# Projecting two chunks of batch 0's keys and values ahead of LayerNorm and the query projection

## The reference

```
x   (8, 64, 512)      ctx (8, 1601, 384)
xn  = layernorm(x)
q   = (xn @ Wq + bq), k = (ctx @ Wk + bk), v = (ctx @ Wv + bv)     # 16 heads of 32
x   = x + softmax(q k^T / sqrt(32)) v @ Wo + bo
x   = x + experts(layernorm(x))                                     # top 2 of 8, hidden 2048
```

## Time and profile before

| | us |
|---|---|
| median of three runs | 1233.47 |
| lowest and highest | 1231.24 and 1234.61 |
| the profiled execution | 1227.9 |
| its span in the trace | 1226.1 |
| PE busy | 1143.8 (93%) |
| DVE busy | 958.2 (78%) |
| ACT busy | 704.6 (57%) |
| POOL busy | 428.0 (35%) |

### The profile page before, as it was taken

How to read it: one execution, slowest core, us unless ns; L and a number is a source line. 1 busy time by engine, 2 the same in 40 slices (tenths; PEclk the granted TensorE clock), 3 DMA queues, 4 the chain that set the end, 5 groups by cost and what they waited for, 6 DMA issues and landing times.

```text
span 1226.1 us, 23151 instructions
## 1 busy us (share of the span) xinstructions
PE 1143.8 (93%) x7488; PEld 1054.2 (86%) x7489; DVE 958.2 (78%) x2082; ACT 704.6 (57%) x1418; POOL 428.0 (35%) x378
## 2 busy tenths in 40 slices
PE   4899999999999999999999998757889999889998
PEld 4799999999999999999999997635668898668897
DVE  6578888888888888888888888865876756876655
ACT  3456656656656656656656656443575565665654
POOL 5454754754654654654664640010000000000000
PEclk9899999999999999999999999966899999989999
DMA  5322122122122122122122103113755634655633
GB/s 181 101 63 62 40 70 61 38 70 61 38 70 61 38 70 61 38 70 61 39 69 61 58 23 118 50 52 105 244 189 184 206 109 164 221 191 193 201 117 103
DMA packets 74304, 121.15 MB, mean 99 GB/s; under 512 B 10776, under 2 KB 35480, under 8 KB 74272
## 3 DMA queue, kind: packets, MB, share of 16 engines
q1 hardware_dynamic: 74272, 120.73, 30.6%
HBM read 118.62 MB, written 2.10 MB: 98 GB/s over the span
## 4 chain that ended last, share of the span: by engine, by line
PE 79%; DVE 9%; ACT 5%; DMA 3%; issue 3%; DVEq 0%; SPq 0%; ACTq 0%
PE ps L401 18%; PE ps L403 17%; PE ps L402 17%; PE ps L1285 7%; PE ps L1337 7%; PE ps L1321 4%; PE ps L1322 3%; DMA w_raw<-in_w_dram 2%; PE ps L1386 2%; DVE w_lo L1027 2%; DVE mx L955 1%; DVE k_mix L877 1%; PE ps L1429 1%; DVE w_lo L1019 1%; PE ps L1430 1%
## 5 line engine op out<-in xcount | busy, mean ns | idle before, releaser
L545 POOL TENSOR_TENSOR ctx_hi<-ctx_raw,no_query 128x1152 fp32r<-128x1152 f32 x64 | 142.8, 2231 | 290.2 <-PE ps L403 281.2
L877 DVE SCALAR_TENSOR_TENSOR k_mix<-ps,bk_sb,k_mix 64x384 fp32r<-64x384 f32 (+1 forms) x256 | 162.3, 634 | 82.1 <-ACT k_mix L644 77.8
L684 ACT ACTIVATE probs<-ps,negmax 128x1152 f32<-128x1152 f32 x64 | 78.3, 1223 | 201.1 <-DVE negmax L958 201.1
L401 PE MATMUL ps<-wv_hi,ctx_hi 128*128 128x256 f32 (+1 forms) x624 | 181.8, 291 | 6.7 <-DVE k_mix L877 6.5
L549 POOL TENSOR_TENSOR ctx_lo<-ctx_raw,ctx_hi 128x1152 fp32r<-128x1152 f32 x64 | 179.7, 2808 | 5.0
L403 PE MATMUL ps<-wv_hi,ctx_lo 128*128 128x256 f32 (+1 forms) x624 | 175.7, 282 | 0.0
L402 PE MATMUL ps<-wv_lo,ctx_hi 128*128 128x256 f32 (+1 forms) x624 | 174.9, 280 | 0.0
L644 ACT ACTIVATE k_mix<-ps,bk_sb 64x384 fp32r<-64x384 f32 (+1 forms) x256 | 150.8, 589 | 24.0 <-PE ps L403 19.4
L969 DVE TENSOR_TENSOR pt_mix<-ps,pt_mix 128x384 fp32r<-128x384 f32 (+1 forms) x256 | 142.2, 580 | 1.4 <-ACT pt_mix L695 1.4
L401 PE MATMUL ps<-ctx_hi,wk_hi 128*128 128x384 f32 (+1 forms) x384 | 133.2, 347 | 0.0
L403 PE MATMUL ps<-ctx_hi,wk_lo 128*128 128x384 f32 (+1 forms) x384 | 132.3, 345 | 0.0
(11 more groups left out here) (219 smaller groups left out, 2668.5 us busy)
## 6 DMA issues: line engine op xcount, KB each, us to landing
w_raw<-in_w_dram SPq DMA_DIRECT2D x68, 1024.0 KB, 5.3
ctx_raw<-in_ctx_t_dram SPq DMA_DIRECT2D x48, 576.0 KB, 3.8
ctx_raw<-in_ctx_t_dram SPq DMA_DIRECT2D x16, 673.5 KB, 4.1
q_both<-q_scratch SPq DMA_DIRECT2D x14, 128.0 KB, 3.1
x<-in_x_dram SPq DMA_DIRECT2D x1, 1024.0 KB, 5.4
wq_raw<-in_wq_dram SPq DMA_DIRECT2D x1, 1024.0 KB, 7.7
q_scratch<-q_out SPq DMA_DIRECT2D x1, 1024.0 KB, 5.4
wo_raw<-in_wo_dram SPq DMA_DIRECT2D x1, 1024.0 KB, 5.4
```

Of the source, the lines that this page charges most:

```text
L401: pe.matmul(acc_ap, a_hi, b_hi, start=start, stop=False)
L545: nc.gpsimd.tensor_tensor(ctx_hi[slot][:, :, 0:n], ctx_raw[slot][:, :, 0:n], no_query[:].rearrange("p (o i) -> p o i", o=1).broadcast_to([ ...
L877: last = nc.vector.scalar_tensor_tensor(out=k_mix[other, 2 * a + i, cols], in0=ps[rows, bank, 0:m], scalar=bk_sb[rows, a:a + 1], in1=k_mix ...
```

## The change

Chunks 0 and 1 of batch 0 are projected first, and LayerNorm and q come after them; chunks 2 and 3 follow q as before. In detail:

- SP issues the biases, Wk, ctx chunk 0, Wv, ctx chunk 1, and then x and Wq. The second loads of chunks 0 and 1 are issued ahead of the store of q.
- ACT copies Wk, chunk 0, Wv and chunk 1 high (the chunks were POOL's), then takes the high parts of chunk 0's units, then Wq, unit 0 of chunk 1, the square root and the table of Exp, the other units of chunk 1, the turned blocks, and chunks 2 and 3, with `qbd_hi` after chunk 2.
- DVE makes Wk low, chunk 0 low, Wv low, then mixes LayerNorm's pieces between the low parts of the ten units; the turned blocks and q follow. `qbd_lo` comes after chunk 2.
- POOL makes chunk 1 low and Wq low (which was DVE's), then chunks 2 and 3.
- PE runs jobs 0 and 1, turns x, makes q, runs jobs 2 and 3. q goes to banks 5, 6, 4 and 7 (`q_bank`).
- The buffers of the start have other places, so that Wq, x and their parts lie where the first units don't write.

```
--- before
+++ after
         first, used[0] = ExitStack(), 0
+        wkv_raw = place("wkv_raw", [P, 2, KC, D], F32, first)
+        pad_to(4 * TILE0[2] * 2 * D, "first_pad0", first)
+        x0 = place("x0", [P, TT, D], F32, first)
+        xn0 = place("xn0", [P, TT, D], F32, first)
         wq_raw = place("wq_raw", [P, KD, D], F32, first)
+        pad_to(4 * (2 * KT * D + STEPS // 2 * NKE), "first_pad1", first)
...
+        def q_bank(m):
+            return (PROJ_BANK + 1, PROJ_BANK + 2, PROJ_BANK, PV_BANK)[m]
...
 # SP
+            sp.dma_start(bk_sb[:], bk_t).then_inc(bias_loaded, 16)
+            sp.dma_start(bq_sb[:], bq_t).then_inc(bias_loaded, 16)
+            sp.dma_start(bv_sb[:], bv_t).then_inc(bias_loaded, 16)
+            sp.dma_start(wkv_raw[:, 0], wk.rearrange("(k p) n -> p k n", p=P)).then_inc(wkv_loaded[0], 16)
+            load_ctx(0, 0, 0)
+            sp.dma_start(wkv_raw[:, 1], wv.rearrange("(k p) n -> p k n", p=P)).then_inc(wkv_loaded[1], 16)
+            load_ctx(0, 1, 1)
             sp.dma_start(x0[:], x_rows).then_inc(x_loaded, 16)
             sp.dma_start(wq_raw[:], wq.rearrange("(k p) n -> p k n", p=P)).then_inc(wq_loaded, 16)
...
 # POOL
             make_norm_tables()
-            for m in range(CHUNKS):
-                split_ctx(m + 1, m, 16 * (m // 2 + 1), UNIT0[m - 1] if m >= 2 else None)
+            pool.wait_ge(ctx_high, 2)
+            pool.wait_ge(ctx_split, 1)
+            nc.gpsimd.tensor_tensor(ctx_lo[1][:, :, 0:KEYS[1]], ctx_raw[1][:, :, 0:KEYS[1]],
+                                    ctx_hi[1][:, :, 0:KEYS[1]].bitcast(F32), ALU.subtract).then_inc(ctx_split, 1)
+            pool.wait_ge(wq_high, 1)
+            nc.gpsimd.tensor_tensor(wq_lo[:], wq_raw[:], wq_hi[:].bitcast(F32), ALU.subtract).then_inc(wq_split, 1)
+            for m in range(2, CHUNKS):
+                split_ctx(m + 1, m, 16 * (m // 2 + 1), UNIT0[m - 1])
...
 # ACT
+            split_first(wkv_raw[:, 0], wk_hi[:], wkv_loaded[0]).then_inc(wkv_high, 1)
+            split_first(ctx_raw[0][:, :, 0:KEYS[0]], ctx_hi[0][:, :, 0:KEYS[0]], ctx_loaded[0]).then_inc(ctx_high, 1)
+            split_first(wkv_raw[:, 1], wv_hi[:], wkv_loaded[1]).then_inc(wkv_high, 1)
+            split_first(ctx_raw[1][:, :, 0:KEYS[1]], ctx_hi[1][:, :, 0:KEYS[1]], ctx_loaded[1]).then_inc(ctx_high, 1)
...
             act.wait_ge(bias_loaded, 48)
-            for c in range(CHUNKS):
+            job_high(None, 0, range(UNITS[0]))
+            split_first(wq_raw[:], wq_hi[:], wq_loaded).then_inc(wq_high, 1)
+            job_high(None, 1, range(KEY_UNITS[0] + 1))
+            act.wait_ge(var_ready, 1)
+            nc.scalar.activation(sd[:], ve[:], ACT.Sqrt).then_inc(sd_ready, 1)
+            warm(ACT.Exp, 1)
+            job_high(None, 1, range(KEY_UNITS[0] + 1, UNITS[1]))
+            for k in range(KD):
+                act.wait_ge(xt_ready, k + 1)
+                nc.scalar.copy(xt0_hi[:, k, :], ps[:, k, :]).then_inc(xt_high, 1)
+            for c in range(2, CHUNKS):
                 job_high(None, c, range(UNITS[c]))
-                if c == 0:
+                if c == 2:
...
 # DVE
+            job_low(None, 0, KEY_UNITS)
+            dve.wait_ge(x_loaded, 16)
+            for t in range(TT):
+                last = nc.vector.bn_stats(stat[:, t, :], x0[:, t, :])
+            step(last)
+            job_low(None, 0, range(len(KEY_UNITS), UNITS[0]))
+            variance()
+            job_low(None, 1, KEY_UNITS[:1])
+            inverse_deviation(1)
+            job_low(None, 1, KEY_UNITS[1:])
+            normal_rows(x0, xn0)
+            job_low(None, 1, range(len(KEY_UNITS), UNITS[1]))
...
 # PE
+            for c in range(2):
+                for k in range(UNITS[c]):
+                    pe.wait_ge(wkv_split, 1 if k in KEY_UNITS else 2)
+                    run_job(None, c, [k])
+            turn(xn0, 0, TT)
+            pe.wait_ge(wq_split, 1)
+            pe.wait_ge(xt_split, KD)
+            pe.wait_ge(proj_split, UNIT0[2])
+            for m in range(KD):
...
+                    last = three_pass(pe, ps[:, q_bank(m), :], ...)
+                last.then_inc(q_ready, 1)
             pe.wait_ge(q_done, KD - 1)
-            for c in range(CHUNKS):
+            for c in range(2, CHUNKS):
                 run_job(None, c, range(UNITS[c]))
```

More of the change, by code:

```diff
@@ L435, in _ @@
                 load_ctx(0, m, m % 2)
+            for c in range(2):
+                sp.wait_ge(ctx_split, CHUNKS - 1 + c)
+                load_ctx(0, c, c % 2)
             sp.wait_ge(q_done, KD - 1)
@@ L626, in _, with split_first @@
             warm(ACT.Sqrt, 0)
-            act.wait_ge(wq_loaded, 16)
-            nc.scalar.copy(wq_hi[:], wq_raw[:]).then_inc(wq_high, 1)
-            act.wait_ge(var_ready, 1)
-            nc.scalar.activation(sd[:], ve[:], ACT.Sqrt).then_inc(sd_ready, 1)
-            warm(ACT.Exp, 1)
-            for k in range(KD):
-                act.wait_ge(xt_ready, k + 1)
-                nc.scalar.copy(xt0_hi[:, k, :], ps[:, k, :]).then_inc(xt_high, 1)
+            def split_first(raw, hi, loaded):
+                act.wait_ge(loaded, 16)
+                return nc.scalar.copy(hi, raw)
+            split_first(wkv_raw[:, 0], wk_hi[:], wkv_loaded[0]).then_inc(wkv_high, 1)
+            split_first(ctx_raw[0][:, :, 0:KEYS[0]], ctx_hi[0][:, :, 0:KEYS[0]], ctx_loaded[0]).then_inc(ctx_high, 1)
+            split_first(wkv_raw[:, 1], wv_hi[:], wkv_loaded[1]).then_inc(wkv_high, 1)
+            split_first(ctx_raw[1][:, :, 0:KEYS[1]], ctx_hi[1][:, :, 0:KEYS[1]], ctx_loaded[1]).then_inc(ctx_high, 1)
             def proj_high_part(unit, n, bank):
@@ L827, in step, with variance @@
                 dve.wait_ge(vector_step, steps[0])
-            def layernorm(src, dst, n):
+            def variance():
                 for t in range(TT):
@@ L1012, in _ @@
                 add_product(t, t + 1)
-            layernorm(acc, xn, 2)
+            variance()
+            inverse_deviation(2)
+            normal_rows(acc, xn)
             def w1_low_piece(group, piece, b=0):
@@ L1234, in _ @@
             pe.wait_ge(psum_zeroed, 1)
-            turn(xn0, 0, TT)
-            pe.wait_ge(wq_split, 1)
-            pe.wait_ge(xt_split, KD)
-            for m in range(KD):
-                for k in range(KD):
-                    last = three_pass(pe, ps[:, 4 + m, :], wq_hi[:, k, m * P:(m + 1) * P], wq_lo[:, k, m * P:(m + 1) * P],
-                                      xt0_hi[:, k, :], xt0_lo[:, k, :], k == 0, k == KD - 1)
-                last.then_inc(q_ready, 1)
             def project(unit, n, bank):
@@ L1269, in run_job @@
                     project(units_of(s if b is not None else CHUNKS + s)[k], n, PROJ_BANK + local % PROJ_BANKS)
-            pe.wait_ge(wkv_split, 2)
+            for c in range(2):
+                for k in range(UNITS[c]):
[5 more added lines that the diff above has]
+            pe.wait_ge(proj_split, UNIT0[2])
+            for m in range(KD):
+                for k in range(KD):
+                    last = three_pass(pe, ps[:, q_bank(m), :], wq_hi[:, k, m * P:(m + 1) * P], wq_lo[:, k, m * P:(m + 1) * P],
+                                      xt0_hi[:, k, :], xt0_lo[:, k, :], k == 0, k == KD - 1)
+                last.then_inc(q_ready, 1)
             pe.wait_ge(q_done, KD - 1)
-            for c in range(CHUNKS):
+            for c in range(2, CHUNKS):
                 run_job(None, c, range(UNITS[c]))
```

63 lines of the change are left out of this document (23 added, 40 removed).

## The result

The changed kernel takes 1240.51 us in the median of five runs (1238.89 to 1241.05), the kernel before, in runs beside it, 1233.14 (1229.85 to 1234.61): a ratio of 1.0075, 95% interval 1.0058 to 1.0092. So the change costs 7.4 us by the medians and 9.2 by the ratio; I had forecast 2.3. The profiled execution's span is 1239.2 us, 13.1 above the one before. Of that, 8.6 us are there when the first scores start (75.36 against 66.74) and 10.0 when the last ones do (789.62 against 779.67 in the two timelines of PE).

The account below looks back on a forecast made before the run. The kernel was taken as bound by TensorE, the change moving only the first scores: q starting at 36.2 put them at 69.0 against 66.74, +2.3 us, so 1233.5+2.3 = 1235.8 us; range 1231 to 1240.5.

Parts of the forecast that it names:

- GpSimd beside DVE: POOL splits chunk 2 while DVE makes LayerNorm's rows (1.85 us): bounds 0 and +2 us, taken as 0.
- covered by 8 us: Wq low on POOL takes 4.55 us instead of DVE's 2.28, but ends at 28.4, 8 us before q needs it.
- Bank wait of chunk 1's unit 0: Ahead of q, chunk 1's first unit waits until value unit 2 low frees its bank at 22.8; PE starts at 23.0.
- Turn: Transposing x ahead of q: 3.9 us at full clock, three value lows before the turned blocks on DVE; q starts at 36.2.
- Landings: When the first loads arrive: Wk at 7.3, chunk 0 at 8.8, x at 15.0, Wq at 17.7; 1 us earlier or 2 later possible.
- The stop at the placing: PE idles while ACT and DVE place q; the stop moves to chunk 3 and stays, 5.3 us, one for one.
- The square root's table: ACT's key units run with Sqrt's table loaded: 0 or one or two more loads of 1.28 us, taken as 0.
- Other homes, passed queues: Moved buffers and reordered loads, stores and POOL or ACT work ahead of the first scores cost nothing.
- Rival 2: LayerNorm's rows on DVE pay up to 2 us beside POOL: +3.3 to +4.2, 1237 to 1238 us; chance 0.10.
- Rival 1: PE's clock falls ahead of q, which runs partly at half clock: +4.3 to +6, 1238 to 1239.5 us; chance 0.22.
- Rivals 3 and 4: 3: tighter front chain, -1.6 to 0 us, chance 0.15. 4: Wk lands only at 10, +5 us, chance 0.03.
- break-even: Latest start of q on PE at which the change costs nothing: 33.9 us, with q ending at 44.8.

Follow-up runs that it names:

- both waits: The changed kernel, but POOL starts Wq low only behind the variance and chunk 2's split only behind LayerNorm's rows: 1235.39 us against 1230.66 for the kernel before.

## Why the prediction was wrong

The forecast was +2.3 us, 1235.8, most likely no difference. It is +7.4 by the medians; 1240.51 is just above the top of the range. The direction was right, the size was not, and the chance of 0.62 for no difference was too high.

**The step that failed** is "GpSimd beside DVE". It asked the right question and bounded it wrongly in three ways. It looked only at LayerNorm's four rows, beside chunk 2's low part; in the run these were free (1.91 us), because POOL was waiting just then (33.01 to 37.09). It left out the six small instructions ahead of them, the variance and the inverse deviation, for which the sum has nothing beyond their order: three of them were held, for 7.0 us. And it read Wv low's 3.66 us as a rate, 2.1 times, which for an instruction of 0.17 us gives 0.2 more; the row means a wait for the end of POOL's instruction, by which the bound is 4.55 us, Wq low's whole length, for every held instruction in turn. The row itself can't tell the two apart; the start and end of POOL's instruction beside it can, and I did not set the two timelines side by side. The choice of 0, "by the nearest row, LayerNorm's own", then rested on a row that ran while POOL was idle, so that it could not show a hold. The page of the Trainium skill that I weighed ("GPSIMD Engine Reference", specifications) says only that there is contention. The rule that gives the size stands in the Trainium skill under "SBUF — State Buffer" ("Who interferes with whom"): a whole instruction, not a share.

Wq low on POOL, "covered by 8 us", is the same mistake from the other side. Its cover held (it ended at 28.24, q began at 41.80): nothing waited for its result. What was not asked is what it does to others while it runs.

**The sum, term by term.** Statistics on DVE at 20.0: 19.83. Bank wait of chunk 1's unit 0: PE at 22.91, forecast 23.0. LayerNorm's rows done at 32.0: 36.48. The holds are 7.0; some 2 of them cost nothing, since DVE waits about that long for ACT where the variance is free (2.04 us with both waits), and the forecast was some 0.5 late without them. (Its 1.85 for the rows is 1.92 in the earlier trace rows, which changes nothing.) Turn of 4.2 us: 5.3, PE at 0.50 of its clock, in the window

```profile
36.90:40.40 3.50, 3.46 (x17) 3.05 (x15) 2.42 (x6) 2.14 (x5) 3.23 (x2) 0.50 0.00 0
```

behind stops of 2.33 and 3.21 us (the timeline of PE above). With both waits there was one stop there, of 2.09, PE was still at 0.50 of its clock from 30.80 to 34.00, and the turn took 4.6. Together these are the 5.6 us. q took 11.3 for 10.9, and from its end to the scores 22.3 for 21.9.

**What held.** *Landings:* Wk landed 4.8 us after issue, and its first copy starts at 7.02 (forecast 7.3); PE starts at 11.70 (12.1), with matmuls at half speed, as forecast. x and Wq come at 10.1 and 12.2 us after issue, and nobody waits for them. The transfers of the first 30 us, beside the earlier trace rows:

```profile
x<-in_x_dram SPq DMA_DIRECT2D x1, 1024.0 KB, 10.1
wq_raw<-in_wq_dram SPq DMA_DIRECT2D x1, 1024.0 KB, 12.2
wkv_raw<-in_wk_dram SPq DMA_DIRECT2D x1, 768.0 KB, 4.8
```

*The stop at the placing:* 4.97 us idle in after, 5.43 before: one for one. *The square root's table:* two table loads in the start, no third, so the 0 was right. *Other homes, passed queues:* nothing waits for them.

**The rivals.** Rival 2 (0.10) was the right pair of engines with the wrong instructions and a price of at most 2. Rival 1 (0.22) came true in part, in the turn and not in q (1.00 over q). The holds made it larger but not alone: with both waits the turn is still 0.4 us above the forecast, at half clock. Rivals 3 and 4 did not happen.

**What the change was worth without the hold.** With both waits it costs 4.7 us by the medians, 4.6 by the first scores, and one instruction was still held for 1.1. So the forecast's sum was low even without its main mistake: q came at 37.17 for 36.2, and q and the rest took 34.1 us for 32.8. The verdict behind the sum, that PE's earlier start is lost on the round trip through PSUM, stands: even with no instruction of LayerNorm held, q starts at 35.93, and could not have before 35.04, when DVE has the last turned block; both are later than my break-even of 33.9. Only the placing in pieces brought the order level. The last 1.3 us are in the trace with both waits: behind the stop at the placing (65.36) the first scores take 5.9 us instead of the 4.9 of the forecast, at a granted clock of 0.50 all the way where I had the third value unit at full clock, and q takes 11.3 instead of 10.9.

**What was not tried:** the changed order with Wq low left on DVE. The run that moved it in the old order shows what the move alone can do, but not what the new order would be without it.

## What to carry to other kernels

Before work is moved to GpSimd, or moved beside it, write down what VectorE runs in that stretch and of which form: of the float32 forms run here, each with two SBUF inputs or from SBUF to SBUF in one source (reciprocal, statistics and reduction excepted) waited for the rest of the GpSimd instruction, 4 us for four elements, however idle both engines look on the page. Price it from the two timelines laid side by side, by ends that coincide, never as a ratio. Where a chain of small instructions leads to the critical path, make GpSimd wait for its end by a semaphore that exists already: this took 4.6 us off q's start in the changed kernel and, with the placing in pieces, 7.2 us off the kernel before. Then look at who waits for GpSimd's late work: where the next stage needed it at once, PE stopped for 2.24 us, and in that trace the gain was gone by the second scores.

## What was not expected of the hardware

- The loser loses again at every instruction: beside a POOL that runs back to back, four rows of 0.54 us take 7.95 us together.
- Beside a POOL memset a TENSOR_TENSOR from SBUF is free (0.15 us), but a TENSOR_SCALAR or COPY is held (1.25 and 1.50 us).
- Holds don't add. Taken away alone they gave 0 and 2.0 us of q's start, together 4.6 (one trace each, the 0 with a unit at half clock in it): an instruction that comes free earlier meets POOL's next one.
- A gain ahead of a dense stretch of PE can be lost to its clock: q at 35.93 instead of 37.68, and 0.85 instead of 1.00 of the clock over it, in one trace of each.
